# A two-layer Fourier kernel: the tables loaded by Pool inside the first pass, and four banks for the last image's turns

## The reference, cut to what matters

```python
def _gn(v, G=32, eps=1e-5):                 # statistics over an image and 2 channels
    g = v.reshape(B_, H_, W_, G, C_ // G)
    return ((g - mean(g)) / sqrt(var(g) + eps)).reshape(v.shape)

def _L0_conv_ref(x, conv, skip_kernel, skip_bias):
    x_ft = rfftn(x, axes=(-3, -2))          # modes 0..15 x 0..15 kept
    out_ft[:16, :16] = einsum('bxyi,xyio->bxyo', x_ft[:16, :16], conv[0] + 1j * conv[1])
    return irfftn(out_ft) + x @ skip_kernel + skip_bias

def _L1_conv_ref(x, fw1, fw2, W, b):
    a = rfft2(x)[:32, :32]                  # 32 x 32 modes, two weight blocks
    out_ft[:32, :32], out_ft[N - 32:, :32] = a * fw1, a * fw2
    out = irfft2(out_ft)
    return relu(out @ W + b + out)

x = x + _L0_conv_ref(_gn(x), ...)
x = x + _L1_conv_ref(_gn(x), ...)
```

## Time and profile before

| | |
|---|---|
| median of 3 executions | 2027.1 us (2022.14 to 2029.2) |
| the profiled execution, its own time | 2027.07 us |
| its span in the trace | 2025.2 us |
| x's first tile issued | 11.02 us |
| the last image's turns begin | 493.03 us |
| the block after the first pass begins | 514.5 us |
| busy: PE, DVE, ACT, POOL | 88%, 69%, 56%, 14% |
| DMA over the span | 536.25 MB, 265 GB/s |

### The profile page before, as it was taken

The page is one execution under the profiler, slowest core; times in us unless marked ns, Lnnn a source line. Parts: engine busy times, 40 slices in busy tenths (PEclk is TensorE's granted clock), DMA queues, the critical chain, the costliest instruction groups (busy, mean ns, idle before and its releaser), DMA issues.

```text
span 2025.2 us, 56232 instructions
## 1 busy us (share of the span) xinstructions
PE 1790.8 (88%) x23806; PEld 1387.8 (69%) x23806; DVE 1401.0 (69%) x2062; ACT 1125.1 (56%) x1841; POOL 293.1 (14%) x548
## 2 busy tenths in 40 slices
PE   5898998998495888885599999999999999999998
PEld 3555665655264777774478878878788787888787
DVE  5886887886635222223678878878788787888787
ACT  5765766665122112112467766667666666677665
POOL 0000000000303000003223040050500504104000
PEclk9998999999655989987799999999999999999999
DMA  8887887883697999994388788888987889878986
GB/s 306 312 290 250 287 292 251 292 290 118 83 165 161 248 258 269 243 240 141 98 298 290 301 314 305 275 304 310 324 311 261 310 307 334 292 276 313 316 322 235
DMA packets 192164, 536.25 MB, mean 265 GB/s; under 512 B 47346, under 2 KB 122610, under 8 KB 156146
## 3 DMA queue, kind: packets, MB, share of 16 engines
q1 hardware_dynamic: 152210, 456.07, 67.4%
q0 software_dynamic: 5376, 43.07, 7.3%
q10 hardware_dynamic: 34336, 33.56, 6.4%
HBM read 355.37 MB, written 144.77 MB: 247 GB/s over the span
## 4 chain that ended last, share of the span: by engine, by line
PE 43%; DMA 9%; DVE 1%; POOL 0%; issue 0%; DVEq 0%; POOLq 0%
PE ps_y L1440 14%; PE ps_xt L1387 10%; PE ps_wave L1426 9%; DMA x_in<-in_x 8%; PE ps_col L1407 5%; PE ps_y L1430 5%; DVE by_channel L808 1%; DVE low_tile L1330 0%; DMA tile<-high_tile 0%; DMA planes_in<-planes 0%; POOL tile L1257 0%; POOL planes_in L1245 0%; DVE by_channel L809 0%; DVE y_out L1359 0%; POOL low_tile L1257 0%
## 5 line engine op out<-in xcount | busy, mean ns | idle before, releaser
L1289 ACT ACTIVATE x_turned<-ps_xt 128x512 f16<-128x512 f32 x512 | 305.6, 597 | 323.7 <-PE ps_xt L1387 323.7
L1440 PE MATMUL ps_y<-apply,x_turned 128*128 128x128 f16 x6144 | 427.9, 219 | 0.0
L1440 PEld LDWEIGHTS ps_y<-apply,x_turned 128*128 128x128 f16 x6144 | 377.2, 98 | 64.5 <-issue 0.6
L1338 DVE TENSOR_TENSOR x_turned<-ps_xt,x_turned 128x512 f16<-128x512 f32 x512 | 351.3, 686 | 98.2 <-ACT x_turned L1289 98.2
L1359 DVE SCALAR_TENSOR_TENSOR y_out<-ps_y,relu 128x512 f32<-128x512 f32 x512 | 351.3, 686 | 21.3 <-PE ps_y L1440 2.8
L223 DVE TENSOR_TENSOR parts<-stage,parts 128x1024 f16<-128x1024 f32 x256 | 301.8, 1220 | 74.0 <-ACT parts L150 74.0
L1387 PE MATMUL ps_xt<-c_eye,x_in 128*128 128x128 f32 x2048 | 311.2, 275 | 14.2 <-DMA x_in<-in_x 14.2
L1299 ACT ACTIVATE relu<-ps_wave 128x512 f32<-128x512 f32 x512 | 303.0, 592 | 14.4 <-PE ps_wave L1426 14.4
L150 ACT ACTIVATE parts<-stage 128x1024 f16<-128x1024 f32 x256 | 254.3, 1048 | 21.8 <-PE gram_ps L315 17.8
L299 PE MATMUL row_ps<-parts,c_rows_dft 128*64 128x512 f16 x1536 | 203.3, 391 | 65.0 <-DVE parts L223 65.0
L1330 DVE SCALAR_TENSOR_TENSOR low_tile<-ps_col,high_tile 128x512 f16<-128x512 f32 x248 | 171.1, 691 | 92.0 <-ACT high_tile L1282 92.0
(11 more groups left out here) (134 smaller groups left out, 1653.5 us busy)
## 6 DMA issues: line engine op xcount, KB each, us to landing
stage<-in_x SPq DMA_DIRECT2D x256, 512.0 KB, 4.9
x_in<-in_x SPq DMA_DIRECT2D x128, 1024.0 KB, 11.1
out_y<-y_out SPq DMA_DIRECT2D x128, 1024.0 KB, 7.0
fw<-in_fw SPq DMA_DIRECT2D x18, 2048.0 KB, 19.5
fw<-in_fw ACTq DMA_DIRECT2D x14, 2048.0 KB, 20.3
tile<-high_tile POOLq DMA_DIRECT2D x48, 240.0 KB, 13.7
planes_in<-planes POOLq DMA_DIRECT2D x8, 1040.0 KB, 20.0
fw<-in_conv SPq DMA_DIRECT2D x8, 1024.0 KB, 15.1
```

What stands on the lines that cost most here:

```text
L1289: nc.scalar.activation(turned[u % 2][:, 0, :, :], ps_turn[u % 2][:, :, :], ACT.Copy).then_inc(turn_high, 1)
L1338: nc.vector.tensor_tensor(v[:, 1, :, :], ps_turn[u % 2][:, :, :], v[:, 0, :, :], ALU.subtract).then_inc(turn_split, 1)
L1440: mm = nc.tensor.matmul(ps_y[u % 2][:, :, 2 * k:2 * k + 2], turned[u % 2][:, p, k, :], apply[:, bass.ds(b, 1), q, :, :].rearrange("p o c w ...
```

## The change

The block of `load_constants` is gone. Its list of transfers is handed to `pass_1`, where Pool issues them, from the block's start on. The first of them, `rows_dft`, has a semaphore of its own, and PE waits for it ahead of its first row products. The other 15 share `constants_landed`; PE waits for all of them at the first turn (`s == 0`) of every image, and Pool itself at the end of its list. So SP's first work is x's first tile.

In the turns of the last image the odd turns go to `row_ps[0]` and `row_ps[1]`, which hold nothing any more then, and the even ones to `turn_ps` as before; a turn from `s = 1` on waits for one copy less. Images 0 to 6 keep two banks.

```diff
-def load_constants(nc, pairs):
-
-    with Memory(nc) as m:
-        landed = m.sem("constants_landed")
-        with nc.Block() as block:
-            @block.sync
-            def _(sp):
-                for dst, src in pairs:
-                    sp.dma_start(dst, src).then_inc(landed, 16)
-                sp.wait_ge(landed, 16 * len(pairs))
...
+        def turn_bank(b, s, i):
+
+            if b is LAST and s % 2:
+                return row_ps[i][:, :, :].rearrange("p w c -> p (w c)").rearrange("p (c n) -> p c n", n=P)
+            return turn_ps[i][:, :, :]
+
+        LAST = B - 1
...
-                nc.scalar.activation(turned[:, :, c:c + TURN_C], turn_ps[0][:, :, :].rearrange("p c n -> p n c"),
+                nc.scalar.activation(turned[:, :, c:c + TURN_C], turn_bank(b, s, 0).rearrange("p c n -> p n c"),
                                      ACT.Copy).then_inc(turn_taken[0], 1)
...
+        @block.gpsimd
+        def _(pool):
+            for n, (dst, src) in enumerate(constants):
+                pool.dma_start(dst, src).then_inc(constants_landed if n else rows_dft_landed, 16)
+            pool.wait_ge(constants_landed, 16 * (len(constants) - 1))
...
                     pe.wait_ge(modes_taken, 2 * b + 2)
+                    pe.wait_ge(constants_landed, 16 * (len(constants) - 1))
                 for i in range(2):
-                    pe.wait_ge(turn_taken[i], b * TURN_STEPS + s + 1)
+                    pe.wait_ge(turn_taken[i], b * TURN_STEPS + s + (0 if b is LAST and s >= 1 else 1))
                     for c in range(TURN_C):
-                        last = nc.tensor.transpose(turn_ps[i][:, c, :],
+                        last = nc.tensor.transpose(turn_bank(b, s, i)[:, c, :],
                                                    rows[parity][:, (2 * s + i) * TURN_C + c, :], eye[:, :])
...
             pe.sem_inc(turn_ready, 2 * TURN_STEPS)
+            pe.wait_ge(rows_dft_landed, 16)
             images(pe, image)
             for s in range(TURN_STEPS):
-                turn(B - 1, 1, s)
+                turn(LAST, 1, s)
```

More of the change, by code:

```diff
@@ L70, in __exit__, with pass_1 @@
         return self.stack.__exit__(*e)
-def load_constants(nc, pairs):
-    with Memory(nc) as m:
-        landed = m.sem("constants_landed")
-        with nc.Block() as block:
-            @block.sync
-            def _(sp):
-                for dst, src in pairs:
-                    sp.dma_start(dst, src).then_inc(landed, 16)
-                sp.wait_ge(landed, 16 * len(pairs))
-def pass_1(nc, B, x, modes, lent, gram, rows_dft, cols_dft, eye):
+def pass_1(nc, B, x, modes, lent, gram, constants, rows_dft, cols_dft, eye):
     with Memory(nc) as m:
@@ L98, in pass_1 @@
         landed = [[m.sem(f"stage_landed{s}_{i}") for i in range(QUADS)] for s in range(2)]
+        rows_dft_landed = m.sem("rows_dft_landed")
+        constants_landed = m.sem("constants_landed")
         high = m.sem("parts_high")
@@ L202, in _ @@
             for s in range(TURN_STEPS):
-                take_turn(B - 1, s)
+                take_turn(LAST, s)
             take_columns(B - 1)
@@ L239, in take_turn @@
                 nc.vector.tensor_copy(turned[:, :, c:c + TURN_C],
-                                      turn_ps[1][:, :, :].rearrange("p c n -> p n c")).then_inc(turn_taken[1], 1)
+                                      turn_bank(b, s, 1).rearrange("p c n -> p n c")).then_inc(turn_taken[1], 1)
             def take_gram(b):
@@ L1530, in two_fourier_layers @@
         w["conv"] = conv
-        load_constants(nc, loads)
         gram = first.sb("gram", [P, B, 2 * C])
@@ L1534, in two_fourier_layers @@
         lent = apply[:, :, :, :, :].rearrange("p b q c w -> p (b q c w)").bitcast(F32)
-        pass_1(nc, B, x, x1, lent, gram, w["rows_dft"], w["cols_dft"], w["eye"])
+        pass_1(nc, B, x, x1, lent, gram, loads, w["rows_dft"], w["cols_dft"], w["eye"])
         with Memory(nc) as mm:
```

## The result

| | before | changed |
|---|---|---|
| median of 6 executions each | 2027.3 us (2022.1 to 2030.0) | 2012.6 us (2009.7 to 2021.3) |
| ratio | | 0.9929, 95% interval 0.9908 to 0.9950 |
| the profiled execution, its own time | 2027.07 | 2012.40 |
| its span | 2025.2 | 2010.6 |

The change gains 14.4 us by the ratio, between 10 and 19 by its interval; 11.9 were forecast, and 2012.6 lies in the stated range. A second set of ten executions of the changed kernel, on another occasion, gave 2012.7 us and a ratio of 0.9932 (0.9911 to 0.9953).

A forecast was written before the change was run, and what follows sets the result against it. The prediction took both places of the change as stretches where one chain runs alone: DMA holds image 0, bank copies hold the last turns. From 2027.07 us, -10.1 + 1.5 + 0.1 - 3.4 = -11.9 gives 2015.2 us, range about 2009 to 2022.

The forecast's parts named there:

- The head: Start of the first pass: x issued 10.1 us earlier, less 1.5 us for the tables' traffic, -8.5 us with the waits.
- The tables' traffic: Tables sharing the DMA engines with x's first tiles: +1.5 us, half of the full 3.2 (0 to 3.2).
- the step under it: Image 0: only delays of the first four tiles count, later ones vanish in eight tiles of prefetch; tile 3's split near 10.5.
- the row of 3.6: Pool's second-pass transfers of 512 KB heading a group take 3.6 us; taken as nearest for rows_dft, so no cost.
- rivals 1 and 3: PE's first matmul: rows_dft late on Pool's queue, 2019.7 us, chance 0.08; Pool's queue starved behind x's, 2030 us, chance 0.03.
- The waits: PE's added wait for the other 15 tables at each image's first turn: 0.1 us, for the last image alone.
- The tail: The last image's eight turns: with two pairs of banks 0.95 us a step instead of 1.44, 3.4 us gained.
- Rival 2: The last image's turns: the four banks bring nothing, something else holds each step; 2018.6 us, chance 0.06.
- The returns: Returns of the loop over image pairs: 3.5 us allowed either way, since each engine's code begins at another place.
- The sum: Whole kernel: -10.1 + 1.5 + 0.1 - 3.4 = -11.9 us, giving 2015.2 us.

The follow-up runs named there:

- the head alone: The change without the four banks: tables issued by Pool, the last image's turns on two banks; ratio 0.9952 against before, 9.7 us less.
- the four banks alone: The kernel before with only the last image's turns on four banks, tables still in their own block; 2023.4 us, ratio 0.9989.

## Why the prediction was right, point by point

**The head.** 10.1 us for the block of the tables: 9.93 measured (first issue at 1.09, not 0.9). The tables' traffic was taken at 1.5, half of the full 3.2: over six kernels with early tables it is 63.3 - 61.8 = 1.5 at the first turn, and 1.8 in the profiled pair. The rule of the Trainium skill's page "DMA: Bandwidth & Descriptors", section "Issuing engines are not separate DMA queues", that transfers share the same engines whoever issues them, holds in kind: the traffic is paid, about half of the 3.2 us. That the half was right is in part luck. It was chosen between two ends, and the step under it was drawn wrongly: tile 3 was 2.0 us late against its issue (its split at 11.53, where the prediction named 10.5), and the doubled traffic left it there, delayed the tiles behind it and cost as much at the first turn: eight tiles of prefetch did not take it up.

**rows_dft.** It landed 4.3 us after its issue, near the row of 3.6 that the prediction took and far from 13.7; rivals 1 and 3 fell. By the figure of the same page of the Trainium skill, section "Anatomy of one DMA — SWDGE (gpsimd) path", 2.0 us plus bytes over 436 GB/s, the other tables of 16 to 128 KB would take an estimated 2.0 to 2.3 us. They took 5.2 to 6.6: beside x's tiles the measurement decides, and it is more than twice that.

**The waits.** No gap at a turn is put down to the tables, the steps of image 0 stayed 6.00 us apart, and PE's idle share in the loop didn't grow. Taken at 0.1 us and not to be seen.

**The tail.** The mechanism held, and the size was a little off: 7 x (1.44 - 0.874) = 4.0 us, not 3.4, since I took 0.95 us a step from between two rows of which the lower, 0.86, was the right one. DVE's first and last copies are 6.12 us apart, just outside the 6.2 to 7.0 that the prediction named as its sign; seven steps of its own lower end would have been 6.0. Rival 2 fell with it, and the third pair of banks confirms that PE and not the copies is the limit. Whether it is PE's weight loads, as the prediction has it, or the transposes was not tried apart.

**The returns.** The allowance of 3.5 us either way was right in size (26.9 to 30.3 us in the same code). Its reason was not, or not alone: I put it down to where each engine's code begins, but the same code varies, by when its fetch starts, and the head alone, whose loop is that of the change, came to 30.2.

**The sum.** -8.1 in the head (forecast -8.5), -4.0 in the tail (-3.4), -1.9 at the first return, -0.6 behind the pass: -14.6 in the span against -11.9. The head is worth 9.93 - 1.5 = 8.4 us over all kernels, so the two edits are worth 8.4 + 4.0 = 12.4 us if the returns are alike; 0.9939 as a ratio, inside both measured intervals. Run alone they gained 9.7 and 2.2 us by their ratios, together 11.9 against the 14.4 of both: with intervals of 3 to 4 us either way that neither confirms nor denies that they add up. The traces do: the head alone brought the first turn 8.5 us earlier (8.1 in the change), and the four banks alone took 0.873 us a step as in the change. Whether the rest of the measured 14 us is chance or belongs to the change stays open: the intervals reach 4 us to either side.

## What to carry to other kernels

Transfers that are not needed at once can be issued by an engine with nothing to do, beside the first data, and cost their traffic and not their block; count what is queued behind the issues, the function table's load too. At the end of a pipeline, banks that the loop used for something else let the last stage run at the rate of its engine. And look at the starts after a hardware loop's return on every engine, and at the DMA packets of kind "instruction" beside them: one return of a long loop body cost PE 5 to 10 us here, more than the four banks gain, and only PE's loop had to be written out.

## What the runs showed that I had not expected

A return of PE's loop stops it for 3.6 to 5.2 us, until 1.6 to 1.7 us after a fetch of 16 KB of code has ended. It mostly stalls PE again for 0.4 to 2.2 us inside a group of matmuls that waits for no one (after the 11th matmul of the group in the code of before, after the 12th in that of the change), and leaves it near 1.2 GHz after that (granted clock 0.54 and 0.58 in windows of the change and of before). The two returns together were 12 to 16 us above ordinary image starts, and differed by 3.4 us between two executions of the same code. Writing PE's loop out gained 14.7 us by the medians and 13.8 by the ratios, as much as the change itself. And where the 0.9 MB of tables doubles, the delay falls on the tiles behind the first four and reaches image 0's first turn all the same, though there is a prefetch of eight tiles.
